# Attention scores on one 64-row half of the TensorE array, with even and odd heads in turn

## What is computed

```python
# B = 16, CH = 128, T = 512, 8 heads of kc = 16 channels
q = Wq @ layernorm(x) + bq ; k = Wk @ ctx + bk ; v = Wv @ ctx + bv     # per batch element [128, 512]
q, k = rope(q, 8), rope(k, 8)                                           # each head, first 8 of 16 channels
scores = einsum('bhqd,bhkd->bhqk', q, k) / sqrt(16)
out = softmax(scores, -1) @ v
x = x + tanh(g_xattn) * (Wo @ out + bo)
# then: x = x + tanh(g_ffn) * rmsnorm(down(silu(gate(layernorm(x))) * up(layernorm(x)))), 4-bit weights, inner size 1408
```

## Time and profile before

| | |
|---|---|
| median of 3 runs | 942.87 us (941.97 to 942.91) |
| span of the profiled execution | 939.5 us (its own time is not listed apart; the runs' median is 3.4 us above the span) |
| PE, DVE, ACT, POOL busy over the span | 880.0, 571.1, 529.1, 220.2 us |
| start, to the first exponential tile on PE | 0 to 60 us |
| steps, with the clock of PE at full speed from 66 us | 60 to 512 us |
| feed-forward | from about 524 us |

### The profile page before, as it was taken

How to read it: one execution, slowest core, us unless ns; L and a number is a source line. 1 busy time by engine, 2 the same in 40 slices (tenths; PEclk the granted TensorE clock), 3 DMA queues, 4 the chain that set the end, 5 groups by cost and what they waited for, 6 DMA issues and landing times. The chain is left out here.

```text
span 939.5 us, 13857 instructions
## 1 busy us (share of the span) xinstructions
PE 880.0 (94%) x4134; PEld 486.0 (52%) x4134; DVE 571.1 (61%) x1024; ACT 529.1 (56%) x991; POOL 220.2 (23%) x196
## 2 busy tenths in 40 slices
PE   4689999999999999999997569999999999999997
PEld 1344544455444445444542356666666666666664
DVE  5878988888888888889994773222322322232112
ACT  3227888788887888887787454224322432252223
POOL 8202343334443343432222750000000000000000
PEclk9559999999999999999999779999999999999999
DMA  6463344444444544344300101000200020001001
GB/s 186 145 183 108 120 121 148 150 126 143 139 127 141 154 127 147 113 130 131 103 25 23 56 1 45 0 1 1 90 1 1 0 89 0 0 2 43 1 1 45
DMA packets 44927, 74.36 MB, mean 79 GB/s; under 512 B 11610, under 2 KB 13914, under 8 KB 44890
## 3 DMA queue, kind: packets, MB, share of 16 engines
q1 hardware_dynamic: 44890, 73.90, 25.6%
HBM read 48.17 MB, written 25.17 MB: 78 GB/s over the span
## 5 line engine op out<-in xcount | busy, mean ns | idle before, releaser
L636 DVE TENSOR_REDUCE row_max<-s_ps 128x1 f32<-128x512 f32 x512 | 330.8, 684 | 61.0 <-PE s_ps L356 57.5
L528 ACT ACTIVATE probs<-st_ps 128x512 f32<-128x512 f32 x512 | 272.8, 599 | 104.6 <-PE st_ps L409 104.1
L356 PE MATMUL s_ps<-k_stack,q_stack 126*128 126x512 f32 x512 | 222.1, 471 | 10.0 <-DMA k_stack<-qk_scratch 9.6
L356 PEld LDWEIGHTS s_ps<-k_stack,q_stack 126*128 126x128 f32 x512 | 100.8, 197 | 148.5 <-DVE row_max L636 87.2
L409 PE MATMUL st_ps<-q_stack,k_stack 128*128 128x512 f32 x512 | 168.0, 408 | 6.2 <-ACT probs L528 3.3
L1113 PE MATMUL gu_ps<-x_head,gu_head 128*128 128x512 f32 x352 | 156.1, 443 | 0.0
L969 DVE TENSOR_TENSOR hidden<-gu_ps,silu 128x512 f32<-128x512 f32 x44 | 30.4, 691 | 202.5 <-ACT silu L1052 202.5
L1052 ACT ACTIVATE silu<-gu_ps 128x512 f32<-128x512 f32 x44 | 26.3, 597 | 204.7 <-PE gu_ps L1116 204.7
L1114 PE MATMUL gu_ps<-x_rest,gu_head 128*128 128x512 f32 x352 | 138.9, 395 | 0.0
L377 PE MATMUL pv_ps<-probs,v_ones 128*32 128x512 f32 x1024 | 136.2, 604 | 0.9 <-ACT probs L528 0.9
L409 PEld LDWEIGHTS st_ps<-q_stack,k_stack 128*128 128x128 f32 x512 | 96.6, 191 | 47.6 <-ACT probs L528 30.2
(11 more groups left out here) (132 smaller groups left out, 935.7 us busy)
## 6 DMA issues: line engine op xcount, KB each, us to landing
qk_scratch<-split SPq DMA_DIRECT2D x32, 512.0 KB, 4.5
k_stack<-qk_scratch SPq DMA_DIRECT2D x192, 64.0 KB, 2.2
q_stack<-qk_scratch SPq DMA_DIRECT2D x64, 128.0 KB, 2.5
xt<-x_dram SPq DMA_DIRECT2D x16, 256.0 KB, 2.9
ct<-ctx_dram SPq DMA_DIRECT2D x16, 256.0 KB, 3.9
cv<-ctx_dram SPq DMA_DIRECT2D x16, 256.0 KB, 2.8
q_stack<-qk_scratch SPq DMA_DIRECT2D x64, 64.0 KB, 2.5
x_res<-x_dram SPq DMA_DIRECT2D x16, 256.0 KB, 5.1
```

The lines of the kernel that those rows point to most:

```text
L356: nc.tensor.matmul(s_ps[n % RING][:], q_stack[p][rows, head, qt * P:(qt + 1) * P], k_stack[p][rows, head // 2, :], start=True, stop=True). ...
L528: nc.scalar.activation(probs[unit % 2][:, slot, k], st_ps[n % RING][:], ACT.Exp).then_inc(expd, 1)
L636: nc.vector.tensor_reduce(row_max[p][:, head, qt:qt + 1], s_ps[n % RING][:], AXIS_X, ALU.max).then_inc(maxed, 1)
```

## The change

`q_stack` is halved: one slot for a pair of heads, the even head's rows in partitions 0 to 47 and its two maximum rows in 48 and 49, the odd one's in 64 to 111 and 112 and 113. No zero rows are left, and their memset goes. Each score matmul of either kind takes only the 48 (or 50) rows of its head, beginning at partition 0 or 64. The tiles are counted so that even and odd heads take turns: S even, ST odd, ST even, S odd in each slot (S: tile for the maxima, ST: for the exponentials). `row_max` is laid out by parity, and the maxima go into `q_stack` with four DMAs of half the size in place of two.

```diff
+DATA_ROWS = 3 * KC
...
+def score_tile(n):
+
+    return 2 * (n // (2 * KT)) + n % 2, n // 2 % KT
+
+
+def weight_tile(unit, slot, k):
+
+    return QUAD * (unit // 2) + 2 * (slot // 2) + 1 - k, 2 * (unit % 2) + slot % 2
...
-        q_stack = [sb(f"q_stack{p}", [P, HEADS, T], F32R) for p in two]
+        q_stack = [sb(f"q_stack{p}", [P, HEADS // 2, T], F32R) for p in two]
...
-        row_max = [sb(f"row_max{p}", [P, HEADS, KT], F32) for p in two]
+        row_max = [sb(f"row_max{p}", [P, 2, HEADS // 2, KT], F32) for p in two]
...
-        WEIGHTS, CONSTS, BLANKS = 16 * 3, 16 * 8, 4
+        WEIGHTS, CONSTS, BLANKS = 16 * 3, 16 * 8, 2
...
             def load_max(sp, b, p):
                 sp.wait_ge(max_neg, b + 1)
-                for r in range(MAX_ROWS):
-                    row = P - MAX_ROWS + r
-                    sp.dma_start(q_stack[p][row:row + 1, :, :].bitcast(F32).rearrange("a h t -> a (h t)"),
-                                 neg_max[p][:, r, :].bitcast(F32)).then_inc(max_in[p], 16)
+                for odd in two:
+                    for r in range(MAX_ROWS):
+                        row = STACK * odd + DATA_ROWS + r
+                        maxima_of = slice(odd * TILES // 2, (odd + 1) * TILES // 2)
+                        sp.dma_start(q_stack[p][row:row + 1, :, :].bitcast(F32).rearrange("a h t -> a (h t)"),
+                                     neg_max[p][maxima_of, r, :].bitcast(F32)).then_inc(max_in[p], 16)
...
             def score(pe, b, p, tiles):
 
-                rows = slice(0, P - MAX_ROWS)
                 for n in tiles:
-                    head, qt = n // KT, n % KT
+                    head, qt = score_tile(n)
+                    rows = slice(STACK * (head % 2), STACK * (head % 2) + DATA_ROWS)
...
-                    nc.tensor.matmul(s_ps[n % RING][:], q_stack[p][rows, head, qt * P:(qt + 1) * P],
+                    nc.tensor.matmul(s_ps[n % RING][:], q_stack[p][rows, head // 2, qt * P:(qt + 1) * P],
                                      k_stack[p][rows, head // 2, :], start=True, stop=True).then_inc(scored, 1)
...
-                            pe.wait_ge(max_in[p], (turn_of(b, p) + 1) * 16 * MAX_ROWS)
-                        head = (unit // 2) * QUAD + slot
+                            pe.wait_ge(max_in[p], (turn_of(b, p) + 1) * 16 * 2 * MAX_ROWS)
                         for k in range(2):
+                            head, kt = weight_tile(unit, slot, k)
+                            rows = slice(STACK * (head % 2), STACK * (head % 2) + DATA_ROWS + MAX_ROWS)
                             n = 2 * (unit * QUAD + slot) + k
                             if not (starting(b, 1) and n < RING):
                                 pe.wait_ge(expd, bank_before(b * TILES + n, n) + 1)
-                            kt = 2 * (unit % 2) + k
-                            nc.tensor.matmul(st_ps[n % RING][:], k_stack[p][:, head // 2, kt * P:(kt + 1) * P],
-                                             q_stack[p][:, head, :], start=True, stop=True).then_inc(st_done, 1)
+                            nc.tensor.matmul(st_ps[n % RING][:], k_stack[p][rows, head // 2, kt * P:(kt + 1) * P],
+                                             q_stack[p][rows, head // 2, :], start=True, stop=True).then_inc(st_done, 1)
...
             def _(pool):
-                for tile in q_stack:
-                    nc.gpsimd.memset(tile[:].bitcast(F32), 0.0).then_inc(blank, 1)
                 for tile in k_stack:
                     nc.gpsimd.memset(tile[:].bitcast(F32), 1.0).then_inc(blank, 1)
```

More of the change, by code:

```diff
@@ L239, in load_half @@
                             rows = stack[p][at:at + (n - 1) * step + 1:step, :, :].bitcast(F32)
-                            if which == 0:
-                                rows = rows.rearrange("c (j two) t -> c j two t", two=2)[:, :, odd, :]
                             sp.dma_start(rows[:, slots, :], src[odd, take, slots, :]).then_inc(half_in[p][h], 16)
@@ L361, in turn_max @@
                 pe.wait_ge(v_ready, b + 1)
-                nc.tensor.transpose(misc_ps[0:HEADS * KT, 0:P], row_max[p][:].rearrange("p h k -> p (h k)"),
+                nc.tensor.transpose(misc_ps[0:HEADS * KT, 0:P], row_max[p][:].rearrange("p o j k -> p (o j k)"),
                                     keep["ident"][:]).then_inc(max_turned, 1)
@@ L527, in scalar_step @@
                                 act.wait_ge(pv_done, b * UNITS + unit - 1)
-                            nc.scalar.activation(probs[unit % 2][:, slot, k], st_ps[n % RING][:], ACT.Exp).then_inc(expd, 1)
+                            head, kt = weight_tile(unit, slot, k)
+                            nc.scalar.activation(probs[unit % 2][:, head % QUAD, kt % 2], st_ps[n % RING][:], ACT.Exp).then_inc(expd, 1)
                         if left >= 3:
@@ L635, in maxima @@
                         dve.wait_ge(max_turned, b - 1)
-                    nc.vector.tensor_reduce(row_max[p][:, head, qt:qt + 1], s_ps[n % RING][:], AXIS_X,
+                    nc.vector.tensor_reduce(row_max[p][:, head % 2, head // 2, qt:qt + 1], s_ps[n % RING][:], AXIS_X,
                                             ALU.max).then_inc(maxed, 1)
@@ L641, in negate @@
                 if not starting(b, 2):
-                    dve.wait_ge(max_in[p], turn_of(b, p) * 16 * MAX_ROWS)
+                    dve.wait_ge(max_in[p], turn_of(b, p) * 16 * 2 * MAX_ROWS)
                 head, rest = neg_max[p][:, 0, :], neg_max[p][:, 1, :]
```

## The result

| | before | after |
|---|---|---|
| median | 942.89 us (4 runs, 941.97 to 943.52) | 931.29 us (4 runs, 929.22 to 933.48) |
| span of the profiled execution | 939.5 us | 931.6 us |
| mean granted clock over it | 0.964 | 0.940 |

The ratio is 0.9873, with a 95% interval of 0.9861 to 0.9886: faster by 11.6 us, clear of the scatter of the runs, where 38 were forecast. It lies in the wide range given for 8 in 10 (890 to 944), and above the range of the case, whose slow end was 922.

What follows compares the result with a forecast made beforehand. PE was taken to set the pace, DVE close behind and next to bind. Twelve steps saving 33.2 us, plus 1.5, 1.3, 0.5 and 1.1 elsewhere, gave 37.6 us: 942.9 to about 905 us, range 890 to 944 (8 in 10).

Steps and rivals of the forecast that it cites:

- the range of the case: Whole kernel if the main forecast's account holds: 890 us with DVE at its floor, 922 with steps of 27.3 us.
- Pairs of row halves: Score matmuls between value groups: full overlap, 1.14 us a piece in place of 2.10, saving PE 7.7 us a step.
- weight loads: Score stream: hidden under the running pair, no cost; as a rival that binds, 912 us or up to 930, chance 0.13.
- The step of 26.0 us: Full attention step: DVE's 24.7 us plus 0.8 for in-order queue stalls and 0.5 for the maxima, against 28.77.
- the signs named beforehand: Trace signs: paired starts, load_max 26 us apart, DVE 95% busy, its idle below 1.5 us, neg_max waits each step.
- the sign against: Attention trace: starts 0.23 us apart or more, PE still at 28.5 us a step, or clock 0.50 behind 66 us.
- they cost nothing: SP's queue: store and load issues behind the maxima move by 1.2 us, covered by load_half's wait for st_done.
- the clock as a rival that holds or not: Attention: a half-empty array might be held at clock 0.50, 220 us more over the whole attention; chance 0.05.
- the sum: Whole kernel's saving: 33.2 + 1.5 + 1.3 + 0.5 + 1.1 = 37.6 us, median to about 905 us.
- The four DMAs: Maxima sent to q_stack: four land just too late for the exponential tile, 0.5 us a step, bounds 0 and 1.3.
- The blocked queue: PE's in-order queue stands at one ring and starves the other: 0.8 us a step, bounds 0 and 2.5.
- The memset's 1.1 us: Start: without the q_stack memset on POOL the first normalisation and the chain to the first score gain 1.1 us.

Runs made afterwards that it cites:

- four issues fewer: Changed kernel with only two of the six k_stack DMAs of each half issued from the third batch element on: 915.2 us (0.9721).
- the same-half pair of runs: Changed kernel with all eight score matmuls of a piece in one row half: 1017 us; the same over all 126 or 128 rows: 943.7 us.

## Why the prediction was right and wrong

**Right.** Pairs of row halves run at once. The Trainium skill's rule (TensorE: Matmul & The Clock Gate, Part 3) holds for them: S and ST start within 10 ns. PE ceased to be the bound, and weight loads bound nothing. The step of 26.0 us is within 0.3 us of what it is once the loads are out of the way (26.2), but by luck, as the sizes below show; in the changed kernel itself it is 27.1. Of the signs named beforehand, the pairs came, and so did the sign against, a clock of 0.50 behind 66 us. DVE was busy for 88% of a step and not 95, its idle before L648 was 3.0 us a step and not below 1.5, and the wait for the DMA from `neg_max` came in the first step and three more, not in each.

**Wrong, the first step: "they cost nothing".** On `load_half` behind the maxima the prediction says that it waits for `st_done` anyway. That is true of its start. Not looked at was who waits for its end. Its ten issues, 6 us, and their landing, 2 more, have to be over before the first maximum tile of the next unit. Before the change that tile came 8 us behind the first issue too (175.22 to 183.26 us), so that the loads fitted just so, and 2.4 us of such waits stood in the trace from 100 to 450 us already. The shorter step uncovered them. It cost 0.9 us a step, 10 us in all, as four issues fewer show.

**Wrong, the second step: the clock as a rival that holds or not.** I gave it 0.05, and thought of a clock that never rises; the sum has every step and the last one at the clock of before, without a reason, and puts nothing on a fall. It fell in the end phase, which alone took 9.7 us more than before in place of 0.5 less, and three times before it, 13.6 us in sum. Two of those lie between 108.69 and 195.51, which took 86.8 us where three steps at full clock take 81.3: 5.5 us. That rows can decide was in no row of the kernel before, where every score matmul covers 126 or 128 of them; the same-half pair of runs shows it for single matmuls. Why pairs lose the clock in one execution and keep it in another stays open.

**Mis-sized.** The four DMAs were given 0.5 us a step. Of 8 KB each they land after 1.9 us instead of 2.7. The first wait for them, given 1.2 us more, is 2.9 us as before; after it PE's weight loads waited for them three times up to the end, 0.4, 0.9 and 1.4 us. The blocked queue was given 0.8 us; with the loads short, a step is 2.3 us above DVE's work, which itself came out at 24.05 instead of 24.7, since its instructions now follow one another more closely (a reduction lasts 680 ns, before 684, but 225 of them cover 141.0 us in place of 146.5). The two errors nearly cancelled, which is why 26.0 looks right. The memset's 1.1 us came to 0.1 at the first score: the first normalisation fell from 1.62 us to 0.55 and PE began at 6.94 us in place of 8.08, but DVE then waited 1.15 us for the second batch element's load, and the first score began at 31.09 us in place of 31.19.

**The sum.** Of the 29.7 us by which the span of the profiled execution missed its forecast, the end took 10.2, the twelve steps 17.8 (late loads some 10, dips of the clock 5.5, the short turns between PE, DVE and ACT, which no run isolates, the rest), and the two after them 2.2. They hold the third dip, at 424 us. The start gave back 0.5. With a clock that holds at the end, as in one trace of six, some 10 us of the miss would be gone.

## What to carry to other kernels

When a change shortens a stage, ask of each transfer in it not only when it may start, but when its last issue lands, and who needs that; a chain that just fitted becomes the new bound. A chain of DMA issues on one queue can be shortened by giving a few to the queue of an engine that is at the right place anyway: the Trainium skill's remark that other queues save only the issue time (Trainium Kernel Development and Optimization, Key Constraints) was worth some 10 us here, for two issues in ten, by the step of 26.2 in place of 27.0 us. The six given to POOL's queue, behind its own work, cost 87. And packing TensorE's rows shortens the work, but the clock was granted less steadily after it: check the granted clock of every stretch, above all where the engine had pauses already, and in more than one execution.

## What was not expected of the hardware

- Matmuls of 48 and 50 rows, one at a time, streaming for 100 us without a pause at clock 0.50, did not raise it; the same matmuls over 126 and 128 rows had it at 1.00 from 64.6 us on. Once it was up, they held it in full steps.
- Pairs of such matmuls in both halves of the rows had the clock up between 65.6 and 79.8 us. In the last step they lost it in four traces of five and kept it in one.
- With one matmul over the whole array behind each two of 50 rows, its results thrown away, the clock stayed at 1.00 through the last step in both traces.
- A DMA issue on ACT's queue ran beside an activation, mostly for 0.32 to 0.50 us, and didn't delay the next one; one in thirty took 1.63 us and delayed it by 1.16.
